# TensorE's signals on a drain behind the matmul instead of on the matmul, in a four-layer graph and expert network

## The chip, the cores and the metric

The kernel runs on one core of one Trainium2 chip. A core has five engines that run their own instruction streams and signal each other with semaphores: TensorE (PE in the profile; its weight loads are PEld, its sequencer PEldq), VectorE (DVE), ScalarE (ACT), GpSimd (POOL) and SyncE (SP). The metric is the time of one execution on the device in microseconds (us); lower is better. Durations below are read from one profiled execution, the times from three timed runs.

## What is computed

The input is x, 6250 nodes of 256 numbers, with 206,250 edges (`src`, `dst`, sorted by `dst`). Four layers follow, each added to x after a layer norm:

```python
x = x + _L0_gnn_ref(_layernorm(x), edge_index, W, att_src, att_dst, bias)     # attention over the edges, 4 heads
x = x + _L0_ffn_ref(_layernorm(x)[None], Wr, br, ...)[0]                      # router, 8 experts, top 2
x = x + _L1_gnn_ref(_layernorm(x), src, dst, edge_weight, W1, b1, W2, b2)     # weighted sum over the edges
x = x + _L1_ffn_ref(_layernorm(x)[None], W_gat, ..., W1, b1, W2, b2, edge_index)[0]  # graph attention picks among 4 experts
```

The two graph layers are gathers and sums over edges: the attention layer forms `h = x @ W`, a factor per edge from `exp(leaky_relu(a_src[src] + a_dst[dst]) - max)`, and sums `factor * h[src]` into `dst`. The weighted layer sums `edge_weight * x[src]` into `dst` and multiplies by two 256 x 256 matrices. The last layer has its own edge list of 131,072 edges and its loops among 8192 nodes, with h only 16 wide: its edge sums give the scores that weigh four dense experts (256 to 512 to 256).

## The kernel before, in words

Nodes are kept in 49 blocks of 128. Edges are worked in tiles of 128, a group (`GRP`) being 8 tiles, and the groups run over a ring (`RINGS`) of buffers. For one tile GpSimd gathers the 128 rows of the edges' sources with one indirect DMA into `G`; VectorE (or VectorE and ScalarE) builds a 128 x 128 matrix `S` that has a one, or the edge's weight, where edge and node of the block meet; TensorE multiplies `S` by `G` into PSUM; VectorE adds the result to the node block in `acc`. All matrix work is in float32, and the trace shows two records for each such matmul.

The stages, with their place in the profiled execution:

- Setup and a plan of the edges, to 105 us; `project_nodes` with the attention weights, 115 to 183 us (projection one).
- `graph_pass` with attention, 253 to 2800 us, 208 groups. GpSimd issues eight gathers a group (`step_attending`, L831) once the sums of the group four before are signalled. TensorE's order for group k (`step_attend`, L1124) is: the eight transposes of group k+1 (L1095), pair sums 2 and 3 of group k-1 (L1115), pair sums 0 of group k, `spread` of group k+1 (eight small matmuls that bring node values to edges, L1105, after `load_registers` at L462), pair sums 1 of group k. Each `pair_sums` (two matmuls) ends with an increment of the semaphore `part`. On `part` wait ScalarE (copies the transposed matrices, L1048, and builds distances for the next ones), VectorE (L944 adds pair sums, L987 takes `spread`'s result) and GpSimd. PSUM has few banks for the sums (`BANKS`), so a pair waits for VectorE's adds of an earlier one (`added`). Transposes and spread have no increment of their own: they are signalled with the pair that follows.
- `finish_attention`, 2800 to 2890 us; projection two (router) to 3040 us, the routing to 3155 us, the eight experts 3160 to 4121 us (another function, not touched), their combination to 4310 us.
- `graph_pass` without attention (weighted), 4314 to 6870 us, 208 groups. TensorE (`step_weighted`, L1138) loads eight registers with the places of the tiles, waits for tiles and one-hot matrices, and makes two halves of four matmuls (L1147), each with an increment of `sum`. VectorE waits on it (L952), and SyncE too: at L819 it counts the sums and lets GpSimd go on (`room`) with its next eight gathers (L839). Towards the end GpSimd also issues scatters (L618) that sort the slots for the last layer.
- `finish_weighted`, 6873 to 7141 us: for each of the 49 blocks, four transposes with an increment of `tr` (L1365), ScalarE copies them out of PSUM (L1351), four matmuls with an increment of `mm` (L1380), VectorE takes the result. GpSimd issues 110 scatters (L618) in the first 139 us of it.
- Projection three, 7154 to 7303 us. In a projection, each block has two transposes (`turn`, L428), a copy by ScalarE, two matmuls (`product`, L440); `turn` of the next block is issued before `product` of this one.
- `slot_pass`, 7320 to 8953 us, 134 groups. TensorE's order for group g (`step`) is: `spread` of group g+1 (L1782, after eight registers are loaded at L1771), then one or two pairs of expert work (`by_w1`, eight matmuls of 128 x 128 x 128 into a hidden tile, L1477, and `by_w2` of the pair before, four matmuls, L1487), then `sums` of group g-1 (L1792, with its own eight registers). A pair is one of 49 node blocks by one of four experts, so there are 196. ScalarE applies gelu (L1496), VectorE moves the results (L1503), GpSimd gathers (L1691).
- `score_and_mix`, to 9074 us.

The order of every engine is written out by hand; a wait on a semaphore stands ahead of the block of instructions that needs it. The instructions of TensorE are dispatched in program order by its sequencer, which also does the register loads. Each `block` ends with a drain on every engine (L135).

Of the kernel before, what the change touches and what calls it, by code (L numbers as in the profile page):

```python
# [289 lines left out]
def project_nodes(sh, tag, stats, weight, ncols, att=None, table=None, table_cols=0, keep=None, keep_from=0,  # L290
# [11 lines left out]
    with Scope(nc) as sc:  # L302
# [123 lines left out]
        @block.tensor  # L426
        def _(pe):
            def turn(it, u):  # L428
                at_least(pe, s["xn"], it * U7 + u + 1)
                if u >= 2:  # L430
                    at_least(pe, s["xt"], it * U7 + u - 1)
                else:
                    at_least(pe, s["xt"], it * U7)
                if turned_rows is not None:
                    at_least(pe, s["kept_turned"], it * U7 + (u - 1 if u >= 2 else 0))
                for c in range(KC):
                    m = pe.transpose(pT[u % 2][:, c, :], XR[:, u, c * P:(c + 1) * P], sh.ident[:, :])
                m.then_inc(s["tr"], 1)

            def product(it, u):  # L440
                i = it * U7 + u
                pe.wait_ge(s["xt"], i + 1)
                for done, used in (("ev", table), ("kept", keep)):
                    if used is not None:
                        at_least(pe, s[done], i - 3 if u >= 4 else it * U7)
                for c in range(KC):
                    m = pe.matmul(pO[u % 4][:, :], XT[:, u % 2, c, :], W[:, c, :], start=(c == 0), stop=(c == KC - 1))
                m.then_inc(s["mm"], 1)

            pe.wait_ge(s["fold"] if att else s["w"], 4 * KC if att else 16)  # L450
            @every_round(pe)
            def _(it):
                turn(it, 0)
                for u in range(U7):
                    if u + 1 < U7:
                        turn(it, u + 1)
                    product(it, u)
# [235 lines left out]
def graph_pass(sh, tag, planned, planned_block, table, width, acc, acc_zeroed, gather_done, rounds0, keep=None, gmax=None,  # L693
# [20 lines left out]
    s = {n: sh.sem(f"{tag}_{n}") for n in names}  # L714
    with Scope(nc) as sc:
# [366 lines left out]
        def _(pe):  # L1082
# [25 lines left out]
            def pair_sums(k, r, pair):  # L1108

                if pair == 0:  # L1110
                    pe.wait_ge(s["pcol"], k + 1)
                pe.wait_ge(s["gp"], k * PAIRS + pair + 1)
                at_least(pe, s["added"], k * GRP + 2 * pair + 2 - BANKS)
                for u in (2 * pair, 2 * pair + 1):
                    m = pe.matmul(pM[u % BANKS][:, 0:width], S[:, r, u, :], G[:, r, u, :], start=True, stop=True)  # L1115
                m.then_inc(s["part"], 1)

            def prefix():

# [18 lines left out]
            def step_weighted(rnd, r):  # L1138
                k = rnd * RINGS + r
                at = places(k)  # L1140
                pe.wait_ge(s["tiles"], k + 1)
                pe.wait_ge(s["onehot"], (k + 1) * GRP)
                for half in range(2):
                    at_least(pe, s["added"], (k - 2) * GRP + (half + 1) * HG)
                    for u in range(half * HG, (half + 1) * HG):
                        rows = G[:, :, :, :].rearrange("p r u d -> p (r u) d")[:, bass.ds(at[u], 1), :]
                        m = pe.matmul(pM[r % 2 * 2 + half][:, u % HG, :], S[:, r, u, :], rows.rearrange("p a d -> p (a d)"),  # L1147
                                      start=True, stop=True)
                    m.then_inc(s["sum"], 1)

            pe.wait_ge(s["loaded"], n_loads)
            if attend:
# [145 lines left out]
def finish_weighted(sh, tag, acc, stats, w1t, w2t, b1, b2, sort, count):  # L1298
# [4 lines left out]
    with Scope(nc) as sc:  # L1303
# [52 lines left out]
        @block.tensor  # L1356
        def _(pe):
            def turn(it, u):
                at_least(pe, s["xn"], it * U7 + u + 1)
                at_least(pe, s["xt"], it * U7 + (u - 1 if u >= 2 else 0))  # L1360
                at_least(pe, s["side"], it * U7 + u + 1)
                for j, rows in enumerate((XR, SR)):
                    for c in range(KC):
                        m = pe.transpose(pT[u % 2][:, j, c, :], rows[:, u, c * P:(c + 1) * P], sh.ident[:, :])
                m.then_inc(s["tr"], 1)  # L1365

            pe.wait_ge(s["w"], 32)
            @every_round(pe)
            def _(it):
                turn(it, 0)  # L1370
                at_least(pe, s["op"], (it - 1) * OPS + 1)
                for u in range(U7):
                    if u + 1 < U7:
                        turn(it, u + 1)
                    at_least(pe, s["xt"], it * U7 + u + 1)
                    for j in range(2):
                        for c in range(KC):
                            m = pe.matmul(out_of(u), XT[:, u % 2, j, c, :], W[:, j, c, :],
                                          start=(j == 0 and c == 0), stop=(j == 1 and c == KC - 1))
                    m.then_inc(s["mm"], 1)  # L1380

        @block.vector
        def _(v):
# [49 lines left out]
class DenseExperts:  # L1433
# [37 lines left out]
    def by_w1(self, pe, i, e):  # L1471
        q = i * self.E + e
        n = len(self.pH)
        at_least(pe, self.s["gelu"], (q + 1 - n) * self.HC)
        for c in range(self.HC):
            for k in range(KC):
                m = pe.matmul(self.pH[e % n][:, c, :], self.W1[:, e, k, c * P:(c + 1) * P],  # L1477
                              self.XT[:, bass.ds(i, 1), k, :].rearrange("p a m -> p (a m)"), start=(k == 0), stop=(k == KC - 1))
        m.then_inc(self.s["h"], 1)

    def by_w2(self, pe, i, e):
        q = i * self.E + e
        n = len(self.pY)
        at_least(pe, self.s["yc"], q + 1 - n)
        pe.wait_ge(self.s["gelu"], (q + 1) * self.HC)
        for c in range(self.HC):
            m = pe.matmul(self.pY[e % n][:, 0:D], self.GT[:, e % 2, c, :], self.W2[:, e, c, :], start=(c == 0),  # L1487
                          stop=(c == self.HC - 1))
        m.then_inc(self.s["y"], 1)

    def gelu(self, a, i, e):
        q = i * self.E + e
# [79 lines left out]
def slot_pass(sh, tag, sort, slot, offset_of, table, ad_at, gmax, pS_all, dense, slot_rows, gather_done, rounds0):  # L1572
# [23 lines left out]
    with Scope(nc) as sc:  # L1596
# [169 lines left out]
        def _(pe):  # L1766
# [7 lines left out]
            def spread(it, g):  # L1774

                k, r = number(it, g), g % RINGS
                at = offsets(k, 0)
                at_least(pe, s["z"], 2 * k)
                pe.wait_ge(s["turned"], k + 1)
                for u in range(GRP):  # L1780
                    nodes = ad_at[:, :, :].rearrange("p a b -> p (a b)")[:, bass.ds(at[u], HEADS)]
                    m = pe.matmul(pA[:, g % 2, u, :], ST[r][:, u, :], nodes, start=True, stop=True)  # L1782
                m.then_inc(s["ad"], 1)

            def sums(it, g):
                k, r = number(it, g), g % RINGS
# [4 lines left out]
                for u in range(GRP):  # L1791
                    m = pe.matmul(pS_all[:, bass.ds(at[u], width)], S[:, r, u, :], G[:, r, u, :], start=False, stop=False,  # L1792
                                  skip_group_check=True)
                m.then_inc(s["sum"], 1)

            def step(it, g):
                if exists(*later(it, g, 1)):
# [10 lines left out]
            for j, out in enumerate(turn_in):  # L1808
                for c in range(4 * j, min(CH, 4 * j + 4)):
                    n = chunk(c)  # L1810
                    m = pe.transpose(out[0:n, (c - 4 * j) * P:(c - 4 * j + 1) * P], slot[:, c * P:c * P + n, 1].bitcast(F32), sh.ident[:, :])
                m.then_inc(s["slots_turned"], 1)
            pe.wait_ge(s["zeroed"], 2)
            pe.wait_ge(s["slots_copied"], len(turn_in))
            spread(0, 0)
# [899 lines left out]
```

## Time and profile before

| what | value |
|---|---|
| time, median of 3 runs | 9087.52 us (9080.73, 9087.52, 9103.37) |
| span of the profiled execution | 9073.9 us |
| TensorE busy | 5819.2 us, 64% |
| GpSimd busy | 5476.3 us, 60% |
| VectorE busy | 3938.2 us, 43% |
| ScalarE busy | 1583.2 us, 17% |
| DMA, mean over the span | 87 GB/s |

The span runs from the first to the last instruction of the profiled execution. No further time of that execution is given beyond it, so it stands beside the median of the runs, which is 13.6 us longer. Busy times are unions of what an engine executes; register, semaphore and DMA-issuing work is not in them, except that GpSimd's indirect transfers are counted while it prepares them. Matmul ends are modelled. "A <- B" in the waits names what ended an idle time; "issue" is time in which the engine waited for nothing that the profile shows.

### The profile page before, as it was taken

To read this page: it belongs to the slowest core of one execution; us is meant where nothing else is said; L and a number is where in the kernel's file an instruction comes from. 1 tells how busy PE (TensorE), PEld (TensorE's weight loads), DVE (VectorE), ACT (ScalarE), POOL (GpSimd) and SP (SyncE) were. 2 spreads that over 40 slices of the span, in tenths; PEclk is the share of its full clock that TensorE was granted. 3 is DMA by queue.
4 is the path that set the end of the run, shared out by engine and by line. 5 is a ranking of instruction groups with operands and counts; after the bars stand their busy time and mean duration, and the time that the engine had idled before them with its cause. 6 is when DMAs were issued, how large, how long until landed. Compare 5 with 4: busy or idle time off the path is not lost. (4 is left out here: it accounts for less than half of the span.)

```text
span 9073.9 us, 116515 instructions
## 1 busy us (share of the span) xinstructions
PE 5819.2 (64%) x27644; PEld 4894.5 (54%) x27645; DVE 3938.2 (43%) x10109; ACT 1583.2 (17%) x3574; POOL 5476.3 (60%) x5690
## 2 busy tenths in 40 slices
PE   4677777777772488881444444444442579998984
PEld 3566665666662477771333333333331478888883
DVE  4566666777776400004444434434331532222225
ACT  1122222221220233330000000000000233333331
POOL 3566666666666466666666666666666246666662
PEclk7777777777775599995777777776765768888786
DMA  3333333333333144443333222222220022222345
GB/s 113 84 88 87 89 89 85 88 86 87 87 86 108 49 140 145 145 145 114 88 89 88 86 81 81 81 80 82 79 82 19 22 60 67 65 69 65 67 67 163
DMA packets 426058, 793.32 MB, mean 87 GB/s; under 512 B 129162, under 2 KB 267134, under 8 KB 425684
## 3 DMA queue, kind: packets, MB, share of 16 engines
q0 software_dynamic: 235504, 474.87, 21.0%
q1 hardware_dynamic: 190436, 317.20, 10.4%
q14 instruction: 84, 0.69, 0.0%
q8 instruction: 34, 0.56, 0.0%
HBM read 720.67 MB, written 70.98 MB: 87 GB/s over the span
## 5 line engine op out<-in xcount | busy, mean ns | idle before, releaser
L1147 PE MATMUL g_pM<-g_G,g_S 128*128 x3328 | 1178.4, 531 | 1570.5 <-DVE g_S L932 834.9
L831 POOL DMA_INDIRECT g_G<-table,X x1664 | 1620.8, 974 | 933.8 <-issue 447.1
L839 POOL DMA_INDIRECT g_G<-table,g_IDX x1616 | 1534.2, 949 | 863.9 <-issue 460.8
L1147 PEld LDWEIGHTS g_pM<-g_G,g_S 128*128 128x128 f32 x3328 | 903.1, 278 | 1845.8 <-issue 1652.9
L1115 PE MATMUL g_pM<-g_G,g_S 128*128 128x260 f32 x3328 | 1196.4, 499 | 593.1 <-DVE acc L944 555.7
L1691 POOL DMA_INDIRECT q_G<-table,slot x1072 | 1037.1, 967 | 591.5 <-issue 288.3
L618 POOL DMA_INDIRECT slots<-sort_PAIR,sort_ADDR x1024 | 1012.3, 989 | 521.4 <-issue 310.7
L952 DVE TENSOR_TENSOR acc<-g_pM,acc 128x256 f32 x1664 | 697.2, 419 | 1257.4 <-remote 693.1
L1115 PEld LDWEIGHTS g_pM<-g_G,g_S 128*128 128x128 f32 x3328 | 722.3, 238 | 906.4 <-DVE acc L944 647.2
L944 DVE TENSOR_TENSOR acc<-g_pM,acc 128x260 f32 x1664 | 711.4, 428 | 468.4 <-remote 204.0
L932 DVE TENSOR_SCALAR g_S<-iota,g_REL,g_WT 128x128 f32<-128x128 f32 x1664 | 588.8, 354 | 288.2 <-issue 259.2
L1105 PEld LDWEIGHTS g_pA<-keep,g_ST 128*128 128x128 f32 x3328 | 555.1, 257 | 80.7 <-issue 69.0
L1477 PE MATMUL q_pH<-ew_XT,ew_W 128*128 (+1 forms) x3136 | 552.6, 347 | 52.9 <-ACT ew_GT L1496 34.6
L1105 PE MATMUL g_pA<-keep,g_ST 128*128 x3328 | 550.1, 297 | 11.9 <-ACT g_ST L1048 1.2
L1477 PEld LDWEIGHTS q_pH<-ew_XT,ew_W 128*128 128x128 f32 x3136 | 514.4, 254 | 71.7 <-ACT ew_GT L1496 42.3
L981 DVE TENSOR_TENSOR g_G<-g_G,g_pF 128x512 f32<-128x512 f32 x832 | 546.6, 678 | 0.3 <-issue 0.3
L1351 ACT ACTIVATE f_XT<-f_pT 128x512 f32<-128x512 f32 x49 | 28.9, 596 | 2804.9 <-issue 2640.8
L2372 PE MATMUL e_pH<-e_XT,e_W 128*128 128x128 f32 x3360 | 410.9, 282 | 164.4 <-ACT e_XT L2316 155.3
L2372 PEld LDWEIGHTS e_pH<-e_XT,e_W 128*128 128x128 f32 x3360 | 391.9, 195 | 204.9 <-ACT e_GT L2333 178.7
L2350 DVE TENSOR_TENSOR e_Y<-e_pY,ew_B 128x256 f32<-128x256 f32 x105 | 44.6, 425 | 924.8 <-PE e_pY L2381 895.2
L1487 PE MATMUL q_pY<-ew_W,ew_GT 128*128 128x256 f32 x1568 | 435.9, 428 | 0.0
L2381 PE MATMUL e_pY<-ew_W,e_GT 128*128 x1680 | 380.3, 379 | 0.7 <-DVE e_Y L2350 0.7
(335 smaller groups left out, 7007.3 us busy)
## 6 DMA issues: line engine op xcount, KB each, us to landing
e_W<-in_L_ffn_W SPq DMA_DIRECT2D x210, 512.0 KB
sort_PAIR<-slot_rows SPq DMA_DIRECT2D x66, 512.0 KB
g_G<-table,X POOLq DMA_INDIRECT x1664
g_G<-table,g_IDX POOLq DMA_INDIRECT x1616
ys_all<-ew_Y SPq DMA_DIRECT2D x196, 128.0 KB
sm_Y<-ys_all SPq DMA_DIRECT2D x28, 896.0 KB, 10.5
q_ST<-slot_rows SPq DMA_DIRECT2D x34, 512.0 KB
sort_ADDR<-slot_rows SPq DMA_DIRECT2D x34, 512.0 KB
```

Source lines behind the costliest of these rows:

```text
L618: pool.indirect_dma_start(self.slots, bass.IndirectOffsetOnAxis(ap=self.ADDR[:, t:t + 1].bitcast(U32), axis=0), self.PAIR[:, t, :], None). ...
L831: pool.indirect_dma_start(G[:, r, u, :], None, table, bass.IndirectOffsetOnAxis(ap=IDX[:, k * GRP + u:k * GRP + u + 1].bitcast(U32), axis= ...
L839: pool.indirect_dma_start(G[:, r, u, :], None, table, bass.IndirectOffsetOnAxis(ap=IDX[:, g * GRP + u:g * GRP + u + 1].bitcast(U32), axis= ...
L932: v.tensor_scalar(S[:, r, u, :], sh.iota[:, :], rel, WT[:, bass.ds(k * GRP + u, 1)], ALU.is_equal, ALU.mult).then_inc(s["onehot"], 1)
L944: v.tensor_tensor(node_sums(blk), pM[u % BANKS][:, 0:width], node_sums(blk), ALU.add).then_inc(s["added"], 1)
L952: v.tensor_tensor(node_sums(blk), pM[r % 2 * 2 + u // HG][:, u % HG, :], node_sums(blk), ALU.add).then_inc(s["added"], 1)
L1105: m = pe.matmul(pA[:, r % 2, u, :], ST[:, u, :], nodes, start=True, stop=True)
L1115: m = pe.matmul(pM[u % BANKS][:, 0:width], S[:, r, u, :], G[:, r, u, :], start=True, stop=True)
L1147: m = pe.matmul(pM[r % 2 * 2 + half][:, u % HG, :], S[:, r, u, :], rows.rearrange("p a d -> p (a d)"), start=True, stop=True)
L1477: m = pe.matmul(self.pH[e % n][:, c, :], self.W1[:, e, k, c * P:(c + 1) * P], self.XT[:, bass.ds(i, 1), k, :].rearrange("p a m -> p (a m)" ...
L1691: pool.indirect_dma_start(G[:, r, u, :], None, table, bass.IndirectOffsetOnAxis(ap=node_of_slot[:, 2 * (k * GRP + u):2 * (k * GRP + u) + 1 ...
L2372: m = pe.matmul(pH[j % 2][:, c, :], W1[:, j, k, c * P:(c + 1) * P], XT[:, j % 2, k, :], start=(k == 0), stop=(k == KC - 1))
```

## The change

Every place in these functions where an increment was attached to the last matmul (or transpose) of a block now issues a drain on TensorE and attaches the increment to that. A drain holds TensorE's sequencer until its older instructions have completed.

```diff
--- before.py
+++ after.py
@@ -435,7 +435,7 @@
                     at_least(pe, s["kept_turned"], it * U7 + (u - 1 if u >= 2 else 0))
                 for c in range(KC):
                     m = pe.transpose(pT[u % 2][:, c, :], XR[:, u, c * P:(c + 1) * P], sh.ident[:, :])
-                m.then_inc(s["tr"], 1)
+                pe.drain().then_inc(s["tr"], 1)
 
             def product(it, u):
                 i = it * U7 + u
@@ -445,7 +445,7 @@
                         at_least(pe, s[done], i - 3 if u >= 4 else it * U7)
                 for c in range(KC):
                     m = pe.matmul(pO[u % 4][:, :], XT[:, u % 2, c, :], W[:, c, :], start=(c == 0), stop=(c == KC - 1))
-                m.then_inc(s["mm"], 1)
+                pe.drain().then_inc(s["mm"], 1)
 
             pe.wait_ge(s["fold"] if att else s["w"], 4 * KC if att else 16)
             @every_round(pe)
@@ -1113,7 +1113,7 @@
                 at_least(pe, s["added"], k * GRP + 2 * pair + 2 - BANKS)
                 for u in (2 * pair, 2 * pair + 1):
                     m = pe.matmul(pM[u % BANKS][:, 0:width], S[:, r, u, :], G[:, r, u, :], start=True, stop=True)
-                m.then_inc(s["part"], 1)
+                pe.drain().then_inc(s["part"], 1)
 
             def prefix():
 
@@ -1146,7 +1146,7 @@
                         rows = G[:, :, :, :].rearrange("p r u d -> p (r u) d")[:, bass.ds(at[u], 1), :]
                         m = pe.matmul(pM[r % 2 * 2 + half][:, u % HG, :], S[:, r, u, :], rows.rearrange("p a d -> p (a d)"),
                                       start=True, stop=True)
-                    m.then_inc(s["sum"], 1)
+                    pe.drain().then_inc(s["sum"], 1)
 
             pe.wait_ge(s["loaded"], n_loads)
             if attend:
@@ -1362,7 +1362,7 @@
                 for j, rows in enumerate((XR, SR)):
                     for c in range(KC):
                         m = pe.transpose(pT[u % 2][:, j, c, :], rows[:, u, c * P:(c + 1) * P], sh.ident[:, :])
-                m.then_inc(s["tr"], 1)
+                pe.drain().then_inc(s["tr"], 1)
 
             pe.wait_ge(s["w"], 32)
             @every_round(pe)
@@ -1377,7 +1377,7 @@
                         for c in range(KC):
                             m = pe.matmul(out_of(u), XT[:, u % 2, j, c, :], W[:, j, c, :],
                                           start=(j == 0 and c == 0), stop=(j == 1 and c == KC - 1))
-                    m.then_inc(s["mm"], 1)
+                    pe.drain().then_inc(s["mm"], 1)
 
         @block.vector
         def _(v):
@@ -1476,7 +1476,7 @@
             for k in range(KC):
                 m = pe.matmul(self.pH[e % n][:, c, :], self.W1[:, e, k, c * P:(c + 1) * P],
                               self.XT[:, bass.ds(i, 1), k, :].rearrange("p a m -> p (a m)"), start=(k == 0), stop=(k == KC - 1))
-        m.then_inc(self.s["h"], 1)
+        pe.drain().then_inc(self.s["h"], 1)
 
     def by_w2(self, pe, i, e):
         q = i * self.E + e
@@ -1486,7 +1486,7 @@
         for c in range(self.HC):
             m = pe.matmul(self.pY[e % n][:, 0:D], self.GT[:, e % 2, c, :], self.W2[:, e, c, :], start=(c == 0),
                           stop=(c == self.HC - 1))
-        m.then_inc(self.s["y"], 1)
+        pe.drain().then_inc(self.s["y"], 1)
 
     def gelu(self, a, i, e):
         q = i * self.E + e
@@ -1780,7 +1780,7 @@
                 for u in range(GRP):
                     nodes = ad_at[:, :, :].rearrange("p a b -> p (a b)")[:, bass.ds(at[u], HEADS)]
                     m = pe.matmul(pA[:, g % 2, u, :], ST[r][:, u, :], nodes, start=True, stop=True)
-                m.then_inc(s["ad"], 1)
+                pe.drain().then_inc(s["ad"], 1)
 
             def sums(it, g):
                 k, r = number(it, g), g % RINGS
@@ -1791,7 +1791,7 @@
                 for u in range(GRP):
                     m = pe.matmul(pS_all[:, bass.ds(at[u], width)], S[:, r, u, :], G[:, r, u, :], start=False, stop=False,
                                   skip_group_check=True)
-                m.then_inc(s["sum"], 1)
+                pe.drain().then_inc(s["sum"], 1)
 
             def step(it, g):
                 if exists(*later(it, g, 1)):
@@ -1809,7 +1809,7 @@
                 for c in range(4 * j, min(CH, 4 * j + 4)):
                     n = chunk(c)
                     m = pe.transpose(out[0:n, (c - 4 * j) * P:(c - 4 * j + 1) * P], slot[:, c * P:c * P + n, 1].bitcast(F32), sh.ident[:, :])
-                m.then_inc(s["slots_turned"], 1)
+                pe.drain().then_inc(s["slots_turned"], 1)
             pe.wait_ge(s["zeroed"], 2)
             pe.wait_ge(s["slots_copied"], len(turn_in))
             spread(0, 0)
```

## Rows read from the trace of the kernel before

**Rows 1.** The page's head and its busy line (engine, busy us, share, instructions).

```profile
span 9073.9 us, 116515 instructions
...
PE 5819.2 (64%) x27644; PEld 4894.5 (54%) x27645; DVE 3938.2 (43%) x10109; ACT 1583.2 (17%) x3574; POOL 5476.3 (60%) x5690
```

**Rows 2.** Windows: stretch, length, busy us (instructions) per engine, PE clock, DMA.

```profile
115.00:183.00 68.00, 59.46 (x294) 48.14 (x294) 44.25 (x155) 18.12 (x49) 14.83 (x50) 0.91 0.30 100
253.00:2800.00 2547.00, 1971.77 (x8251) 1544.11 (x8250) 1716.71 (x3623) 504.69 (x867) 1605.84 (x1648) 0.76 0.32 85
2892.00:2965.00 73.00, 13.40 (x58) 11.32 (x58) 32.30 (x153) 4.92 (x11) 51.78 (x54) 0.50 0.43 131
2965.00:3040.00 75.00, 49.33 (x236) 46.52 (x236) 34.87 (x150) 15.21 (x40) 15.37 (x17) 0.50 0.01 1
...
4314.00:6870.00 2556.00, 1178.04 (x3328) 902.70 (x3327) 1041.47 (x3315) 0.00 (x0) 1661.57 (x1745) 0.71 0.29 83
6873.00:7012.00 139.00, 26.76 (x88) 20.52 (x88) 10.19 (x29) 4.18 (x7) 105.47 (x110) 0.57 0.04 7
7012.00:7141.00 129.00, 97.14 (x498) 83.48 (x499) 79.78 (x142) 35.74 (x54) 0.16 (x1) 0.89 0.00 0
...
7320.00:8950.00 1630.00, 1463.57 (x8981) 1388.39 (x8979) 450.16 (x1137) 608.89 (x1316) 1036.16 (x1071) 0.81 0.31 66
```

**Rows 3.** Timeline of POOL, attention pass: start, us, what, [idle before <- releaser].

```profile
1545.03 0.95 POOL L831 DMA_INDIRECT g_G<-table,X  x1 [0.30 <-issue]
1546.28 0.95 POOL L831 DMA_INDIRECT g_G<-table,X  x1 [0.30 <-issue]
```

**Rows 4.** Grouped rows of POOL, weighted pass, then attention pass.

```profile
L839 POOL DMA_INDIRECT g_G<-table,g_IDX x1607 | 1525.6, 949 | 841.1 <-issue 458.4 <-SPq L819 382.7
...
L831 POOL DMA_INDIRECT g_G<-table,X x1632 | 1590.5, 975 | 924.2 <-issue 437.5 <-PE g_pM L1115 363.7 <-remote 122.9
```

**Rows 5.** Waits: engine, line <- releaser: us in total, times, longest.

```profile
DVE acc L952 <- remote: 693.1, 115, 13.7
...
ACT g_ST L1048 <- remote: 303.1, 61, 6.1
```

**Rows 6.** Timeline of PE and ACT, the same stretch of the attention pass.

```profile
1534.97 2.29 PE L1115 MATMUL g_pM<-g_G,g_S 128*128 128x260 f32 x8 [0.44 <-issue]
...
1544.11 2.29 PE L1115 MATMUL g_pM<-g_G,g_S 128*128 128x260 f32 x8
...
1536.30 1.02 ACT L1048 ACTIVATE g_ST<-g_pT 128x1024 f32<-128x1024 f32 x1 [1.48 <-PE g_pM L1115]
...
1548.94 1.02 ACT L1048 ACTIVATE g_ST<-g_pT 128x1024 f32<-128x1024 f32 x1 [4.97 <-remote]
```

**Rows 7.** Timeline of PE and ACT in the weighted finish.

```profile
6908.09 0.63 PE L1364 MATMUL f_pT<-ident,f_SR 128*128 128x128 f32 x2
...
6933.54 0.60 ACT L1351 ACTIVATE f_XT<-f_pT 128x512 f32<-128x512 f32 x1 [29.50 <-issue]
```

**Rows 8.** L1378 on PE, 6873 to 7012 and 7012 to 7145: ns min/median/max, first and last.

```profile
L1378 PE MATMUL f_pO<-f_W,f_XT x56: 379/634/796, 6884.2 to 7004.5; 128*128 128x256 f32 x56
...
L1378 PE MATMUL f_pO<-f_W,f_XT x336: 379/379/635, 7030.5 to 7141.4; 128*128 128x256 f32 x168
```

**Rows 9.** L135 around the weighted pass's end, and PE's timeline there.

```profile
L135 PEldq DRAIN  x1: 5730/5730/5730, 6864.2 to 6864.2; - x1
...
6863.32 6.59 PE L1147 MATMUL g_pM<-g_G,g_S 128*128 x16 [9.92 <-issue]
```

**Rows 10.** Slot pass: timeline of PE, L1792 from 8016 to 8024, and the loads of L1771.

```profile
8020.50 1.86 PE L1792 MATMUL slot_sums<-q_G,q_S 128*128 128x20 f32 x16
...
L1792 PEld LDWEIGHTS slot_sums<-q_G,q_S x16: 190/192/192, 8020.3 to 8022.1; 128*128 128x128 f32 x16
...
L1792 PEldq FUSED_REGOPS  x8: 37/37/37, 8018.6 to 8019.7; - x8
...
L1771 PEldq TENSOR_LOAD <-offset_of x268: 587/592/843, 7321.2 to 8945.4; - x134
```

## The prediction, made before the change was run

> **What bounds the kernel now.** The page's head and busy rows come first: a span of 9073.9 us in which TensorE (PE) works 64% and GpSimd (POOL) 60%; no engine bounds the whole [rows 1]. So I go stage by stage with the windows view [rows 2]. In the attention graph pass (2547 us) PE is busy 1972, in the weighted graph pass (2556 us) only 1178, in the slot pass 1464 of 1630. The slot pass is PE's; the graph passes are something else's. That something is POOL: in a burst it issues one gather each 1.25 us [rows 3], so a group of eight needs 10.0 us, while a group takes 2547 / 208 = 12.25 and 12.3 us. Its grouped rows say why: it waits on PE's sums, 364 + 123 us in the attention pass, and 383 us through SP in the weighted one [rows 4].
>
> Now the waits view [rows 5]: VectorE (DVE) waits 693 us before L952, which adds PE's sums, on "remote", and ScalarE (ACT) 303 us before L1048. "Remote" stands where the trace finds nobody that has just finished. The timeline shows what it is [rows 6]. PE runs two pairs of sums from 1534.97 to 1537.26, and ACT's copy starts at 1536.30, behind the first of the two. In the next group the same two pairs run from 1544.11 to 1546.40, but ACT's copy starts at 1548.94: some 3.5 us late, 1.7 us after the last gather issue of POOL's burst (1546.28 + 0.95 [rows 3]). So **a signal that rides on a matmul comes late while POOL's indirect transfers are under way**. The weighted finish shows it at its largest: PE's transposes end at 6908.72, ACT's next work starts at 6933.54, while POOL issues scatters [rows 7]. In the 139 us with scatters 7 tiles are finished (56 matmul records at 8 a tile), in the 129 us without 42 (336) [rows 8], POOL being busy 105 us and 0.2 [rows 2]. The first projection has little of it: POOL is busy 15 of 68 us [rows 2].
>
> **The change part by part.** It takes the increment off the last matmul of a block and puts it on a drain: 294 in three projections, 832 and 416 in the two graph passes, 98 in the weighted finish, 392 + 268 + 3 in the slot pass, 2303 in all. No DMA and no other engine's instruction moves.
>
> *What a drain costs PE.* The one of its kind in the trace is the block's end, L135 [rows 9]. PE's sequencer sits in it from 6864.2 for 5.730 us, to 6869.9, when the last matmul of L1147 ends (6863.32 + 6.59 = 6869.91), within 0.1 us. So a drain blocks the sequencer, and nothing behind it is dispatched ahead. Price of one where PE has work waiting: a matmul ends 0.16 us after the point at which the next could start (L1792: sixteen of 0.266 us in 1.86 us are one start per 0.106 us), the drain itself some 0.05, and the next weights, now not loaded ahead, 0.19 [rows 10]: **0.40 us**. Bounds: 0.05 (the drain alone) and 0.6 (as much again as the weights for a fresh start).
> The Trainium skill (TensorE: Matmul & The Clock Gate, Part 2, step 5 and "Single matmul latency") has a lone matmul pay 166 to 183 ns that a stream hides; as an estimate from that page, 2303 x 0.17 = 0.39 ms, before anything is set against idle time.
>
> *Register loads.* Before spread and before sums of the slot pass (L1771), before spread of the attention pass (L462) and before each group of the weighted pass PE's sequencer loads eight registers: 0.59 us, and eight register operations of some 0.045 [rows 10]. Today it does so ahead: L1792's operations run from 8018.6, its first matmul at 8020.50. Behind a drain it can't. Price 0.59 + 0.36 = **0.95 us** each where exposed; bounds 0 and 1.2.
>
> *Slot pass, 134 groups.* 663 / 134 = 4.9 drains x 0.40 + 2 x 0.95 = 3.9 us a group, on the path. PE's idle 166 us, 1.24 a group, can cover as much: 2.6 x 134 = **+350**. Ends 0 (drains alone, all in the idle) and +650 (0.6 and 1.2 each, mostly uncovered).
>
> *Attention pass, 208 groups.* Four drains, 1.6, and a load, 0.95: 2.55 us a group. The late signals: I take the 3 us gap of [rows 6] for every second group, which is 104 x 3 = 312 us or 1.5 a group; ACT's 303 us on "remote" are its mark, the trace naming other releasers for the rest [rows 5]. Without them 12.25 - 1.5 = 10.75 us. PE's idle is 575 / 208 = 2.8 a group, less the 1.5 leaves 1.3 as cover: 10.75 + 2.55 - 1.3 = 12.0, 208 x -0.25 = **-50**. Ends: -250 (all covered; POOL's 10.0 is next) and +220 (10.75 + 2.55, nothing covered).
>
> *Weighted pass, 208 groups.* Two drains and a load, 1.75 us a group, lie in 1378 us of idle PE, 6.6 a group; were that cover gone they would cost 364 us. The gain is bounded by POOL, which issues 208 x 8 gathers and 138 scatters at 1.25 us, 2253 us: 2556 - 2253 = 303. Its 383 us behind SP's L819 (SP counts the late sums before it makes room) are more than that. I take **-230**; ends -300 and 0.
>
> *Finish and projections.* Finish: with prompt signals 49 tiles at 129 / 42 = 3.07 us are 151, and 98 drains x 0.40 are 39, against 268 now: **-80**; POOL's 110 scatters run beside in 139. Projection two does 13.4 us of PE work in its first 73 us, beside POOL's scatters, then 49.3 in 75 [rows 2], the same lateness; projection three is alike: I take **-60** for both, ends -100 and 0. Projection one has nothing to win, 98 drains at 0.25 on the mean: **+25**.
>
> Sum: 350 - 50 - 230 - 80 - 60 + 25 = **-45**, a span of 9029. The median of the runs, 9087.5, is 13.6 above the profiled span: 9042, said as **9040**.
>
> What the trace of before can't show is whether a drain's signal is itself prompt while POOL transfers; where drains stand (L135) POOL has none under way. The sum takes it as prompt: the lateness is in the array's own report, and the drain's increment is the sequencer's. The Trainium skill (PSUM — Partial Sum Buffer, "Engine vs sequencer instructions") advises the opposite of this change: put the increment on the producing matmul, which signals on completion, and keep a drain for a barrier, as it waits until the engine is idle. The trace does not agree that such a signal comes at completion: 3.5 and 25 us late [rows 6, 7].
>
> **The rivals.** *One: the slot pass decides, slower.* Prompt signals too, but PE's idle there is no cover, since it waits for other engines at other moments: 134 x 3.9 = +520, attention pass +100 for the same reason, weighted pass -150, the rest -115: +355, 9440. For it: PE is busy 90% there [rows 2]. It decides once more than some 3.0 us a group stay uncovered (the +45 that the others leave beyond my 2.6). *Two: the drain's completion is held like the matmul's.* Then PE itself stops for each late one, where today it runs on. In the attention pass it would stand until POOL's burst ends, 10 us and some 5 of its own work, +2.7 x 208 = 560; in the slot pass 5 us a group more, +670; weighted pass +200: about 10,500. Against it only the argument above. *Three: little happens.* The drain costs 0.05 and the late ones wait for the landing of the transfers, whoever sends them: within 0.3%. *Four: more than the sum*, slot pass at a third of its price, graph passes at their low ends: 120 - 250 - 300 - 80 - 60 + 25 = -545, 8540; counted with the forecast.
>
> **How the numbers follow.** Forecast with four 0.49, rival one 0.27, two 0.16, three 0.08. The forecast's own range is 8540 to 9060. Low 8560; up through rival one with upper terms (650 + 220 - 230 - 80 - 60 + 25 = +525, 9610) to 9620; rival two is what is left out. Faster by over 0.3% (27 us, about what a measurement of this kernel can tell from no change) 0.49, within 0.08, slower 0.43.
>
> **What would show it.** In the windows view of after: over 30 tiles in the finish beside the scatters, not 7; the weighted pass under 2400; the "remote" waits of DVE and ACT nearly gone; the slot pass near 1980, with gaps on PE of 0.4 behind L1477 and 1.3 before L1782 and L1792, each drain ending with its matmul. Wrong if the "remote" waits stay and PE's drains last 2 us and more in every burst (rival two), or if the slot pass is unchanged (three) or over 2150.

## The result, and the profile after

The changed kernel takes 10,568 us (median of 4 runs, 10,541 to 10,573) against 9,091 before (4 runs): a ratio of 1.162, 95% interval 1.160 to 1.165. It is slower by 1,477 us, where 45 us less was forecast and 9,620 was the upper end of the range. The profiled execution's span is 10,571.4 us.

The page's head and its busy line, after (before: [rows 1]):

```profile
span 10571.4 us, 118818 instructions
...
PE 6603.1 (62%) x27644; PEld 5154.6 (49%) x27645; DVE 3973.2 (38%) x10109; ACT 1586.7 (15%) x3574; POOL 5474.4 (52%) x5690
```

TensorE's busy time rose by 784 us (6603 - 5819) though its instructions are the same 27,644. The windows view of the changed kernel, each stage from its first to its last instruction (before: [rows 2]; its columns are length, then busy us of PE, PEld, DVE, ACT and POOL, the granted clock of PE, DMA share and GB/s):

```profile
129.00:248.00 119.00, 92.04 (x294) 50.99 (x294) 39.74 (x145) 18.83 (x49) 0.00 (x0) 0.82 0.16 53
268.00:3169.00 2901.00, 2155.07 (x8324) 1549.31 (x8324) 1744.85 (x3652) 509.89 (x875) 1629.18 (x1681) 0.68 0.28 76
4721.00:7381.00 2660.00, 1232.54 (x3328) 852.35 (x3327) 1046.29 (x3315) 0.00 (x0) 1663.42 (x1745) 0.70 0.27 79
7394.00:7540.00 146.00, 34.51 (x108) 23.91 (x107) 17.37 (x34) 7.77 (x12) 102.14 (x103) 0.57 0.02 1
7540.00:7675.00 135.00, 114.10 (x481) 80.22 (x479) 70.00 (x127) 32.43 (x49) 0.00 (x0) 0.93 0.00 0
7903.00:10451.00 2548.00, 1936.38 (x8992) 1706.46 (x8991) 455.03 (x1133) 609.50 (x1316) 1030.94 (x1063) 0.67 0.18 42
```

The slot pass is the bulk: 2548 us for 1623, its PE busy 1936 for 1466 and its granted clock 0.67 for 0.81. Its row before, from first to last instruction as above:

```profile
7330.00:8953.00 1623.00, 1465.97 (x8992) 1391.11 (x8992) 448.33 (x1133) 608.89 (x1316) 1028.58 (x1063) 0.81 0.30 65
```

The attention pass, from its first gather (at 203 us before) to its last sum, went from 2598 to 2901, its clock from 0.76 to 0.68; the weighted pass from 2556 to 2660. Where POOL scatters in the finish, 146 us still hold only 108 TensorE matmuls (103 scatters), as 139 us held 88 before. The first projection doubled, 61 to 119 us; the two others went from 122 to 163 and from 120 to 158.

The waits view, after (before: [rows 5]):

```profile
ACT ew_GT L1496 <- PEq L1479: 1381.7, 158, 23.4
POOL q_G L1691 <- PEq L1794: 1205.5, 130, 19.8
...
DVE acc L952 <- PEq L1149: 1089.2, 267, 13.4
...
POOL g_G L831 <- PEq L1116: 787.3, 204, 10.2
...
POOL g_G L839 <- SPq L819: 481.8, 103, 11.2
```

"Remote" is gone by name, since the drain now stands there as releaser, but the waits are not: L952 waited 693 us on "remote" and now 1089 us on the drain, and POOL's waits rose from 383 to 482 through SP and from 364 + 123 to 787 on L1115's sums. What such a drain looks like, in the timeline of the weighted pass (PE, then the one drain of L1149 in that stretch, then DVE):

```profile
5520.32 3.77 PE L1147 MATMUL g_pM<-g_G,g_S 128*128 x8 [4.21 <-issue]
5529.15 3.78 PE L1147 MATMUL g_pM<-g_G,g_S 128*128 x8 [5.05 <-issue]
...
L1149 PEldq DRAIN  x1: 8128/8128/8128, 5520.7 to 5520.7; - x1
...
5528.99 0.42 DVE L952 TENSOR_TENSOR acc<-g_pM,acc 128x256 f32 x1 [6.76 <-PEq L1149]
```

The eight matmuls end at 5524.09. The drain that began at 5520.7 takes 8.128 us and ends at 5528.85, **4.8 us late**; DVE starts 0.14 us later, and TensorE, which before would have run on to its next half, stands still until 5529.15. Over the stage a third of the 416 drains (135) end more than 0.5 us behind their last matmul; all together come 839 us behind. The drain's own signal arrives 13 ns behind its end. So what comes late is not the signal's way but the completion that TensorE reports.

### The profile page after: what moved, and what is told of

It reads as the page before. It is cut to its first block and busy times, and to the rows that moved or that the text cites. A ratio compares the mean times of both kernels' runs of the same rounds, so it can differ in the third digit from the quotient of the medians.

```text
span 10571.4 us, 118818 instructions
## 1 busy us (share of the span) xinstructions
PE 6603.1 (62%) x27644; PEld 5154.6 (49%) x27645; DVE 3973.2 (38%) x10109; ACT 1586.7 (15%) x3574; POOL 5474.4 (52%) x5690
## 5 line engine op out<-in xcount | busy, mean ns | idle before, releaser
L1147 PE MATMUL g_pM<-g_G,g_S 128*128 x3328 | 1233.0, 534 | 1619.3 <-issue 927.5
L1147 PEld LDWEIGHTS g_pM<-g_G,g_S 128*128 128x128 f32 x3328 | 852.8, 269 | 1999.4 <-issue 1844.0
L1115 PE MATMUL g_pM<-g_G,g_S 128*128 128x260 f32 x3328 | 1370.9, 553 | 228.1 <-issue 205.7
L952 DVE TENSOR_TENSOR acc<-g_pM,acc 128x256 f32 x1664 | 696.2, 418 | 1347.2 <-PEq L1149 1089.2
L1115 PEld LDWEIGHTS g_pM<-g_G,g_S 128*128 128x128 f32 x3328 | 818.0, 272 | 606.6 <-issue 393.3
L944 DVE TENSOR_TENSOR acc<-g_pM,acc 128x260 f32 x1664 | 712.1, 428 | 457.2 <-PEq L1116 313.7
L1477 PE MATMUL q_pH<-ew_XT,ew_W 128*128 (+1 forms) x3136 | 628.2, 381 | 49.4 <-issue 47.9
L1487 PE MATMUL q_pY<-ew_W,ew_GT 128*128 128x256 f32 x1568 | 529.0, 496 | 197.6 <-issue 197.5
L1477 PEld LDWEIGHTS q_pH<-ew_XT,ew_W 128*128 128x128 f32 x3136 | 580.6, 286 | 95.7 <-issue 93.9
L1105 PE MATMUL g_pA<-keep,g_ST 128*128 x3328 | 444.6, 266 | 281.1 <-issue 279.9
L1105 PEld LDWEIGHTS g_pA<-keep,g_ST 128*128 128x128 f32 x3328 | 427.4, 207 | 375.7 <-issue 375.7
L1095 PE MATMUL g_pT<-ident,g_S 128*128 128x128 f32 x1664 | 408.2, 427 | 247.3 <-issue 232.1
L1487 PEld LDWEIGHTS q_pY<-ew_W,ew_GT 128*128 128x128 f32 x1568 | 371.2, 249 | 303.8 <-issue 241.4
L1095 PEld LDWEIGHTS g_pT<-ident,g_S 128*128 128x128 f32 x1664 | 326.7, 224 | 379.3 <-issue 356.5
```

What stands on the lines that cost most here:

```text
L944: v.tensor_tensor(node_sums(blk), pM[u % BANKS][:, 0:width], node_sums(blk), ALU.add).then_inc(s["added"], 1)
L1095: m = pe.transpose(pT[:, u, :], S[:, r, u, :], sh.ident[:, :])
L1105: m = pe.matmul(pA[:, r % 2, u, :], ST[:, u, :], nodes, start=True, stop=True)
```

## The experiments

The fifteen runs were taken in four groups, the kernel before beside each, and it did not take the same time: 9,079 us in the first group (four runs), 7,613, 7,611 and 7,603 us in the three others. Times are therefore compared within a group.

### One stage at a time, and what of a drain costs

Only the slot pass has drains (663 of them: L1479, L1489, L1783, L1794, L1812).

> Drains only in the slot pass (663 of the 2303: L1479, L1489, L1783, L1794, L1812); all else as before. Theory A (each stage pays for itself: PE's sequencer stops, the register loads and the restart are exposed and the granted clock falls): the slot pass lasts 2550 us as with all drains, instead of 1623, the other stages as before, whole about 10,015 us (+926). Theory B (the slot pass is slow with all drains because the stages ahead of it leave it something, such as a low clock): the slot pass stays under 2200 us, whole under 9,700.

Measured: 10,005 us against 9,079, the slot pass 2544 us, all other stages as before. Theory A holds to 10 us.

Only the attention pass (L1116, 832 drains):

> Drains only in the attention graph pass (832, L1116). Theory A: that pass goes from 2548 to about 2900 us, whole about 9,440 us (+350), and the drains end on time (0.02 us behind the last matmul) in three of four cases and 0.5 to 1.5 us late in the fourth. The rival that prompt signals give the pass something back (my forecast's term of -50): whole 9,040.

Measured: 9,369 against 9,079, ratio 1.031 (1.024 to 1.038); the stage went from 2598 to 2895 us between its first and last instruction. That is 70 us less than expected, and far from the 9,040 of the rival. Of the 832 drains 172 end over 0.5 us late; all together come 260 us behind. No gain is left in the stage.

The signals stay on the matmuls, and a drain without a signal stands behind each, slot pass only (one of the five places shown):

```diff
-        m.then_inc(self.s["h"], 1)
+        m.then_inc(self.s["h"], 1)
+        pe.drain()
```

> Slot pass only: the increments stay on the matmuls as before, and a drain without an increment is added behind each. Theory A (the stop costs, not who sends the signal): as with the moved signals or somewhat worse, slot pass 2550 us or more, whole 10,015 to 10,200. Rival (the drain's own signal path costs): close to before, under 9,500.

Measured: 9,989 us, slot pass 2544. Who sends the signal makes next to no difference (10,005 with the signal moved, 0.2% apart); the stop is the cost, and nothing is gained by moving.

Two drains in a row at each place, the second with the signal:

> Slot pass only, two drains in a row at each place, the second with the increment. Theory A (a drain on an idle array is nearly free, the stop behind it is what costs): 663 x 0.05 = +33 us over the single drains, about 10,050. Rival (a drain has a price of its own of 0.4 us or more, whatever stands before it): 663 x 0.4 = +265 us, 10,280 or more.

Measured: 10,027 us, 22 us over the single ones. In the trace the second ends 0.078 us behind the first. The instruction is nearly free; what TensorE may not do behind it is the cost.

### The same kernels where completions are on time

From here on the runs met another condition, which I call the second, and the one so far the first. It is not tied to a chip's number: the record gives chip 0 for the first group (9,079 us) and for the second (7,613), and chips 8 and 10 for the others (7,611 and 7,603). Whether number 0 was the same piece both times is not on record.

> The kernel before, signals on the matmuls, with 105 of GpSimd's 110 scatters taken out of the weighted finish and issued during the experts instead (6 for each expert tile, not 5, as far as the scatters of the sort go). Theory H (a matmul's completion is reported late while GpSimd's indirect transfers are under way): without scatters the finish runs all 49 tiles at the 3 us of its quiet part, 150 to 165 us instead of 260, and the experts, whose TensorE is busy 83%, stay at 961 to 1000; whole 8,960 to 9,010. Rival (the finish's slow start has another reason, such as its first loads or the low clock): the finish stays over 220 us and the whole within 0.5% of before.

```diff
-            experts(..., sort, 5)
+            experts(..., sort, 6)
-            finish_weighted(..., a["L1_gnn_b1"], a["L1_gnn_b2"], sort, 110)
+            finish_weighted(..., a["L1_gnn_b1"], a["L1_gnn_b2"], sort, 5)
```

Measured: 7,729 us against 7,613, ratio 1.016 (1.014 to 1.018). It could not decide, because here the kernel before itself ran in 7,613. With all drains added:

> All 2303 drains, with the same scatters moved. Theory H says that a drain's end is held as a matmul's signal is, so without scatters the finish loses its stretch of 146 us for 9 tiles: 49 tiles at 135/40 = 3.4 us, about 165 to 175 us instead of 282, no drain of L1365 or L1380 over 0.5 us late after the first few; whole about 10,460. Rival (drains in the finish are late for their own reason): the finish stays near 280.

Measured: 9,105 us; finish 164 us, and not one drain at any of the 2303 places over 0.5 us late, beside gathers too: each ends 0.02 us behind its last matmul. The kernel before once more, for its trace:

> The kernel before once more, for its trace. The call before this one gave 7,613 us for it, not 9,079, and the drains of that call ended 0.02 us behind their last matmul at every place, beside transfers of GpSimd too. Theory H (on the chip of the first runs TensorE's completion is reported late beside GpSimd's indirect transfers, on that of the last call it is not, and the 1,466 us are the price of that): if the time is near 7,613, no signal of L1115 or L1147 is over 0.5 us late; if near 9,080, 60 to 80% are. Rival (the time of the last call has another reason, such as the clock): late signals are as frequent at 7,613 as at 9,080.

Measured: 7,600 us. The windows view of this run (slot pass last):

```profile
191.00:2340.00 2149.00, 1721.37 (x8324) 1338.20 (x8324) 1727.08 (x3652) 509.63 (x875) 1618.18 (x1680) 0.86 0.38 103
2455.00:2516.00 61.00, 60.68 (x294) 57.87 (x293) 46.69 (x201) 18.77 (x49) 46.36 (x49) 0.50 0.51 156
2615.00:3420.00 805.00, 787.67 (x5248) 723.15 (x5248) 44.15 (x104) 313.36 (x1049) 602.87 (x625) 1.00 0.55 169
3605.00:5802.00 2197.00, 1205.38 (x3328) 923.16 (x3327) 1033.92 (x3316) 0.00 (x0) 1665.79 (x1745) 0.74 0.34 96
5820.00:5952.00 132.00, 114.26 (x588) 98.14 (x588) 87.53 (x162) 39.81 (x61) 102.42 (x98) 0.96 0.02 1
...
6090.00:7478.00 1388.00, 1347.70 (x8992) 1287.40 (x8992) 438.45 (x1134) 608.94 (x1316) 1017.81 (x1064) 0.87 0.49 76
```

and its waits view, with the lines that stood for late signals in [rows 4, 5]:

```profile
DVE acc L952 <- PE g_pM L1147: 998.2, 260, 13.3
...
POOL g_G L831 <- PE g_pM L1115: 28.2, 39, 3.6
```

All 49 tiles of the finish are done in 132 us while POOL issues its scatters (102 us busy) in the same stretch; before it was 7 tiles in 139 us. The attention pass takes 2149 us for 2598, the weighted pass 2197 for 2556, the experts 805 for 961, and POOL waits 28 us on L1115 where it waited 364 + 123. Every matmul signal of L1115, L1147, L1477, L1487, L1792 comes 13 to 15 ns behind its modelled end. In the first trace, of the signals that it holds, 31% of L1115's came over 0.3 us late, 59% of L1147's, 75% of L1477's and 85% of L1487's. A wait alone doesn't tell of lateness: L952 waits 998 us here, where every signal is on time, and waited 693 + 314 before. A gather's issue (0.946 us at the median), a DVE add (0.428) and a matmul of L1477 (0.275) last the same in both traces. So what Theory H expects is found: **TensorE's completions come late in the first condition and on time in the second, and the kernel before takes some 1,470 us more in the first**; no drain cures it. That all of the 1,470 us are the price of lateness rests on having found no other difference in the work: the packets of the gathers' queue last 0.156 us at the median in both.

What makes completions late stays open, and one rival stands untested: the recording itself. The six traces of the first condition hold 40,000 to 46,000 semaphore updates, the eleven of the second 122,000, for nearly the same instructions; of the 1664 adds at L952 the first trace has the update of 923, the second of all. The consumers did start late (DVE at 5528.99 above), so the lateness is more than a gap in the records. But every timed run on record has a recorded span and clock, so none shows whether TensorE is late when nothing is recorded.

> All 2303 drains once more. If this chip shows late signals: 10,570 us. If not: the last call's run with moved scatters gives 9,105, less what moving cost there (116 of 7,729 - 7,613), so about 9,000: slot pass 2,245, attention 2,497, weighted 2,213 us. In both cases 1,390 to 1,500 us over before.

Measured: 8,970 us against 7,611 (a single run; 18% slower). Its windows view:

```profile
243.00:2743.00 2500.00, 1997.63 (x8324) 1463.76 (x8324) 1735.17 (x3652) 509.67 (x875) 1630.90 (x1681) 0.77 0.33 89
2858.00:2966.00 108.00, 80.75 (x294) 59.22 (x293) 47.99 (x201) 18.82 (x49) 51.03 (x54) 0.50 0.29 88
...
4048.00:6244.00 2196.00, 1199.34 (x3328) 835.87 (x3326) 1041.20 (x3316) 0.00 (x0) 1664.99 (x1744) 0.77 0.34 96
6262.00:6426.00 164.00, 138.90 (x587) 98.16 (x586) 87.50 (x161) 40.24 (x61) 106.37 (x103) 0.93 0.02 1
...
6602.00:8847.00 2245.00, 1804.30 (x8992) 1615.27 (x8992) 455.91 (x1134) 608.89 (x1316) 1030.33 (x1063) 0.73 0.21 47
```

Beside the rows above this is the change without any lateness in it: the weighted pass hides its drains wholly (2196 for 2197), the attention pass pays 351 us, the slot pass 857, the finish 32, projection two 47. The runs with moved scatters and with the remaining stages alone, in the same group:

> The scatters of the weighted finish moved to the experts, signals on the matmuls. Where signals come late: finish 150 to 165 us instead of 260, experts up to 130 us longer, whole within 1% of before. Where they do not: finish 132 us, no gain, 1.6% slower than before, as in the last call.

Measured: 7,739 us, ratio 1.016 (1.013 to 1.019); finish 133, experts 938 for 805 us. Moving the scatters costs the experts more than the finish has to give here; what it gives where signals are late wasn't measured.

> Drains in the weighted pass, the weighted finish and the three projections only (808). Where signals come late: weighted pass 2,660 us (+104), finish +23, projections +136, whole +265. Where they do not: the weighted pass hides its drains and stays at 2,209 (+5), finish about +30, projections +45 to +60 each, whole +170.

Measured: 7,766 us, ratio 1.020 (1.017 to 1.023); weighted pass 2198, finish 162, the three projections 119, 108 and 109 for 60, 61 and 67. With the attention pass's 351 and the slot pass's 857 its 155 us make 1,363; the whole change measured 1,359 (8,970 - 7,611).

### What the 857 us of the slot pass are

Dense drains alone, and the two others alone:

> Drains only behind by_w1 and by_w2 (392, L1479 and L1489) in the slot pass; spread and sums signal from the matmul. Theory A by gaps (L1479: late by 155 us in sum and 0.21 before the next matmul, L1489: 1.16 us before sums' registers, spread's load hidden again): +155 + 392 x 0.16 + 196 x 0.21 + 134 x 1.16 = 415 us, some 100 to 200 more for the clock: 9,600 to 9,700. If each of the 663 drains cost the same 926/663 = 1.4 us: 392 x 1.4 = 550, 9,630; if the two drains beside the register loads carry nearly all: under 9,450.

> Slot pass, drains behind spread and sums alone (268, L1783 and L1794). One register load is exposed a group (spread's, behind the drain of sums; that of sums stays ahead, behind by_w2). By gaps: 134 x (0.18 + 1.28) + 134 x (0.18 + 0.2) = +247 us. With dense alone at +563 (1,951 - 1,388) and all at +857, parts that add up want +294. Clock theory: 300 or more, granted clock under 0.82. On a chip with late signals the same over 1,623.

Measured: 8,167 (ratio 1.073, 1.071 to 1.075) and 8,177 us (1.075, 1.072 to 1.079), slot pass 1951 and 1955 for 1388. Their costs of 563 and 567 us sum to 1,130, not 857. By the count used below, gaps and uncovered ends are 302 and 218 us of them (the expectations had 260, its 155 for lateness aside, and 247 by gaps) and nearly add up to the 520 of both together. What doesn't add up is the slower pace inside the streams, 261 and 350 us alone and 337 together. By_w1's drain alone:

> Slot pass, drains behind by_w1 alone (196, L1479), which no register load follows. Stop without a load: 196 x (0.16 + 0.02 + 0.21) = +76 us if only the gaps count; slot pass 1,388 + 76 = 1,465 where signals come on time. Clock theory (a gap on TensorE also lowers the granted clock, and the streams behind it run at half pace): up to twice that, 1,540, with a granted clock under 0.85 against 0.87.

Measured: 7,672 us, ratio 1.009 (1.006 to 1.012), slot pass 1455: +67 us for 196 drains, **0.34 us each**. The windows of the slot pass in the three runs, by_w1 alone first, then spread and sums alone, then dense alone (read the granted clock, third from the end):

```profile
6091.00:7546.00 1455.00, 1391.77 (x8991) 1294.65 (x8991) 445.25 (x1133) 608.85 (x1316) 1030.77 (x1064) 0.87 0.45 73
```

```profile
6098.00:8053.00 1955.00, 1743.99 (x8992) 1642.16 (x8991) 456.88 (x1133) 608.84 (x1316) 1029.83 (x1063) 0.69 0.24 54
```

```profile
6094.00:8045.00 1951.00, 1703.34 (x8992) 1526.06 (x8992) 452.39 (x1133) 608.88 (x1316) 1026.99 (x1064) 0.76 0.25 54
```

At 0.34 us a drain the clock stays at 0.87. Once a register load is exposed behind a drain it falls to 0.76 and 0.69. The line L1477 in the page's form, of the kernel before in this condition and of the one with drains at spread and sums alone, which are not even at L1477 (ns min/median/max):

```profile
L1477 PE MATMUL q_pH<-ew_XT,ew_W x3136: 272/275/562, 6097.5 to 7459.2; 128*128 x180, 128*128 128x128 f32 x16
```

```profile
L1477 PE MATMUL q_pH<-ew_XT,ew_W x3136: 272/421/578, 6106.1 to 8029.7; 128*128 x180, 128*128 128x128 f32 x16
```

Its matmuls last 0.421 us at the median for 0.275, and their starts follow each other after 0.213 us for 0.112: the same stream at 1.2 for 2.4 GHz. The timeline of the changed kernel's slot pass in this condition shows the two side by side:

```profile
7303.95 1.97 PE L1487 MATMUL q_pY<-ew_W,ew_GT 128*128 128x256 f32 x8 [0.23 <-issue]
7307.21 1.96 PE L1792 MATMUL slot_sums<-q_G,q_S 128*128 128x20 f32 x16 [1.30 <-DVE q_G L1744]
7310.50 3.52 PE L1782 MATMUL q_pA<-ad_at,sort_PAIR 128*128 x16 [1.33 <-issue]
7314.23 3.55 PE L1477 MATMUL q_pH<-ew_XT,ew_W 128*128 x16 [0.22 <-issue]
7318.02 1.96 PE L1487 MATMUL q_pY<-ew_W,ew_GT 128*128 128x256 f32 x8 [0.23 <-issue]
```

Behind L1487 PE idles 1.30 us, and L1792 still takes 1.96 us for its sixteen matmuls. Behind L1792 it idles 1.33 us, and the two streams that follow take 3.5 us for sixteen; L1487 after them is back at 1.96 for eight, as before the gaps. Of the 857 us: gaps between streams are 440 us for 40 (+400), the starts within the streams sum to 1574 us for 1237 (+337, all of it clock, since at full clock one start follows another after 0.111 or 0.216 us in both runs), and 120 us are the ends of 663 matmuls that nothing overlaps now, 0.18 each. The load on its own:

> Drains in the slot pass as in the run with those alone (10,005 us), but the eight registers for the sums are loaded ahead of the drain of spread, where TensorE is still busy. Register theory (0.95 us exposed at each of 134 loads): the gap before L1792 falls from 1.19 us to 0.2 to 0.3 us, whole 10,005 - 125 = about 9,880, and some 20 to 60 us more if the clock recovers. Rival (the load is not what the gap holds, the drain or a wait is): 9,990 to 10,010.

```diff
                     m = pe.matmul(pA[:, g % 2, u, :], ST[r][:, u, :], nodes, start=True, stop=True)
+                loaded = offsets(number(*ahead), 1) if ahead else None
                 pe.drain().then_inc(s["ad"], 1)
+                return loaded
...
-                at = offsets(k, 1)
+                at = loaded or offsets(k, 1)
```

Measured: 8,258 us; slot pass 2033 against 2245 with all drains. The gap before L1792 fell from 1.18 to 0.32 us (115 us over 132 gaps), and the streams came to 1481 us for 1574: of 212 us one register load gave 115 as time and 92 as clock. The other way round, a stage at full clock that the change left out:

> Drains in the experts alone (L2364, L2375, L2383: 4 a tile, 420), which the change left out; TensorE is busy 98% there at a granted clock of 1.00 and loads one register before by_w2 of a tile. By gaps: 420 x 0.4 = 168 us and 105 loads of 1 us, 105 us: 805 + 273 = 1,080 where signals are on time. Clock theory: if the clock stays at 0.97 or more the 1,080 hold, if it falls under 0.9 the stage is 1,200 or more.

Measured: 7,849 us, ratio 1.032 (1.029 to 1.035); experts 1044 us for 805, granted clock 1.00. Here 420 drains and 105 single register loads cost 239 us, 12% under the 273 of the prices, with nothing on top: where the clock holds, the prices are all.

## Why the prediction was wrong

**"The sum takes it as prompt: the lateness is in the array's own report, and the drain's increment is the sequencer's"** is the step that failed. The report is late, and a drain's end is late with it: 839 us in sum over the weighted pass, 270 over the attention pass. The sum had taken gains of 312, 230, 117 and 60 us from prompt signals (attention, weighted, finish, two projections), some 720 of the 1,540 us by which the stages missed it; none of them came. **The second step that failed is the slot pass**, 575 us more than its +350: PE's idle was taken as cover, and the granted clock was put at nothing without a reason.

Rival two named this first step, and its figure (about 10,500) is within 1% of the result, but that is luck: its terms were +560, +670 and +200 for the attention, slot and weighted pass, measured +303, +925 and +104, and its mechanism, TensorE held at each late drain, is not where most of the time went. In the second condition, where no drain is late, the change costs 1,359 us of the 1,477 all the same. The prices of a stop, of an exposed load and of the clock make them up. It had 0.16 for the sole reason that the argument quoted above looked like evidence; nothing in the trace supported it, so the two cases deserved like chances.

**The weighted pass** (-230): +104. In the condition of the forecast 839 us of late drains stand where late signals stood, and PE's stop is added. Its other half, that the two drains and the load hide in PE's idle time, was right: 2196 us for 2197 where completions are on time.

**The attention pass** (-50, 12.0 us a group): 13.9. The mechanism had two parts. The second condition's 2500 / 208 = 12.02 us a group looks like the forecast's 12.0 and is luck: the base there is 10.33 us, not 10.75, and stops and load add 1.69 net of cover, not 1.25. The 1.5 us a group of late signals that were to vanish did not; 270 us of late drain ends remain, and there are four stops a group to meet them.

**The slot pass** (+350, ends 0 and 650): +925, beyond both ends. Price by price: 0.40 us a drain measured 0.34 (of it "some 0.05" for the drain itself, which no row before shows, and 0.03 by the doubled drains), the load 0.95 measured 0.86 as time. Drains and loads alone were put at 3.9 us a group or 523 us uncovered, and 400 + 120 = 520 us are what gaps and ends cost where completions are on time. Two terms were wrong. PE's idle was taken as cover for 166 us and covered nothing: PE's idle went from 157 to 612 us in the first condition. And the clock was left out altogether: +337 us in the second condition, +341 in the first (its other terms there are 455 for the idle and 129 for the ends). The page's line of granted clocks (0.81 in this stage, [rows 2]) was the place to ask what longer gaps would do to it.

**Finish and projections** (-80, -60, +25): +23, +79, +58. Late completions stayed, so no gain; and 98 drains in a chain TensorE, ScalarE, TensorE, VectorE cost 0.4 to 0.6 us each rather than 0.25.

Of the two statements of the Trainium skill that were weighed, the one on restarts (0.39 ms, TensorE: Matmul & The Clock Gate, "Single matmul latency") gave a cost where my sum gave a small gain, but on its own would have stayed at a quarter of the 1,477 us. The advice to keep a drain for a barrier (PSUM — Partial Sum Buffer, "Engine vs sequencer instructions") was the better guide to the result than my reading of the late signals; that a matmul's signal comes on completion agrees with the second condition (13 to 15 ns) and not with the first.

## What to carry to other kernels

A drain instead of a matmul's own signal costs TensorE some 0.35 us each time that it has work waiting, 1.2 us where a load of eight registers stands behind it, and in the slot pass, which TensorE bounds, two thirds as much again in clock (337 on 520 us); put one only where TensorE idles anyway. Late completions were not mended here by changing who reports them, since the drains ended late too. And before a stage's time is explained from one trace, it is worth asking whether the lateness in it belongs to the kernel or to the condition in which it ran: a second trace of the same kernel at another time, and a count of the records in both, would have shown it.

## What was not expected of the hardware

- The kernel before takes 9,079 to 9,091 us in the first condition and 7,603 to 7,613 in the second, with the same durations of a gather's issue, a DVE add and a matmul at full clock. What differs is the lateness of TensorE's completions beside GpSimd's indirect transfers, up to 25 us in the first, 13 to 15 ns in the second. Completions of VectorE's adds (L944, L952) and ScalarE's copies (L1048) are some 10 ns behind in both, as far as the first trace has them.
- Adding a stop changes the pace of streams that have no stop in them: L1477's matmuls went from 0.275 to 0.421 us at the median through drains at L1783 and L1794. Gaps of 0.9 us among the experts left the clock at 1.00; gaps of 1.3 us in the slot pass went with 0.69 to 0.76.
- A second drain directly behind a first costs 0.078 us in the trace, 0.03 us by the time of the whole kernel.
